# Building the expert row lists one choice at a time: both one-hot tiles on GpSimd instead of one on GpSimd and one on VectorE and ScalarE

## The reference

```python
xn = _layernorm(x)
# attention, per batch
qkv = einsum('bsd,ed->bse', xn, Wqkv_w) + Wqkv_b
scores = where(causal, einsum('bqhd,bkd->bhqk', q, k) * scale, min)
out = einsum('bsd,ed->bse', softmax(scores) @ v, out_w) + out_b
# experts, over the 2048 rows
probs = softmax(xn @ w_router.T)
top_w, top_e = top_k(probs, 4); top_w /= sum(top_w)
for e in range(16):
    coeff = sum(where(top_e == e, top_w, 0))
    ffn += coeff * ((silu(xn @ w_gate[e]) * (xn @ w_up[e])) @ w_down[e])
return x + out + ffn
```

## Time and profile before

| | us |
|---|---|
| median of 3 runs | 504.1 (502.85 to 505.03) |
| the profiled execution | 504.1 |
| its span, first to last instruction | 502.4 |
| TensorE busy | 418.8 (83%) |
| GpSimd busy | 294.8 (59%) |
| VectorE busy | 226.0 (45%) |
| ScalarE busy | 179.8 (36%) |

### The profile page before, as it was taken

The page is one execution under the profiler, slowest core; times in us unless marked ns, Lnnn a source line. Parts: engine busy times, 40 slices in busy tenths (PEclk is TensorE's granted clock), DMA queues, the critical chain, the costliest instruction groups (busy, mean ns, idle before and its releaser), DMA issues.

```text
span 502.4 us, 6742 instructions
## 1 busy us (share of the span) xinstructions
PE 418.8 (83%) x1672; PEld 227.8 (45%) x1673; DVE 226.0 (45%) x555; ACT 179.8 (36%) x424; POOL 294.8 (59%) x298
## 2 busy tenths in 40 slices
PE   4896083888889888879899999999999999999920
PEld 2242031434544544435565555555555555555510
DVE  5987688468767666413232222222222222222210
ACT  2353100337745556633333333333333333333310
POOL 7953130998511100303888888888888888888740
PEclk9889555559999999999999999999999999999985
DMA  7668796344876792642544444454544455446217
GB/s 218 228 180 189 179 131 97 126 80 136 167 151 165 179 187 86 213 147 64 78 76 81 82 79 77 77 82 76 84 74 75 84 85 82 75 77 81 38 22 146
DMA packets 54034, 57.17 MB, mean 114 GB/s; under 512 B 11376, under 2 KB 48928, under 8 KB 53760
## 3 DMA queue, kind: packets, MB, share of 16 engines
q0 software_dynamic: 15440, 21.51, 25.6%
q1 hardware_dynamic: 25904, 22.87, 20.9%
q10 hardware_dynamic: 12672, 12.58, 8.4%
HBM read 37.40 MB, written 23.33 MB: 121 GB/s over the span
## 4 chain that ended last, share of the span: by engine, by line
PE 36%; issue 19%; POOL 16%; DVE 12%; DMA 8%; SPq 4%; ACT 3%; ACTq 0%; POOLq 0%
POOL late L512 10%; PE bank L785 9%; PE bank L801 5%; PE bank L664 4%; PE bank L638 4%; PE bank L653 4%; POOL odd_d L526 3%; PE bank L692 3%; DVE pmax L1194 3%; POOL out_dram L526 3%; DMA late<-xn_d,get_row 2%; PE bank L676 2%; DVE early L1051 2%; PE bank L775 2%; DMA q_d<-early 2%
## 5 line engine op out<-in xcount | busy, mean ns | idle before, releaser
L785 PE MATMUL bank<-wgu,late 128*128 x316 | 152.2, 604 | 3.0 <-issue 1.2
L512 POOL DMA_INDIRECT late<-xn_d,get_row x79 | 83.2, 1053 | 69.2 <-PE bank L653 27.6
L1285 DVE SCALAR_TENSOR_TENSOR late<-late,bank 128x256 f32<-128x256 f32 x79 | 37.9, 480 | 154.5 <-ACT late L986 154.5
L925 ACT ACTIVATE pt<-bank 128x512 f32<-128x512 f32 x96 | 56.0, 599 | 79.3 <-PE bank L653 78.3
L801 PE MATMUL bank<-wdn,late 128*128 x316 | 81.5, 381 | 1.4 <-DVE late L1292 1.4
L1194 DVE TRANSPOSE_TENSOR_REDUCE pmax<-bank 128x16 f32<-128x512 f32 x96 | 66.5, 706 | 33.7 <-PE bank L638 32.7
L986 ACT ACTIVATE late<-bank 128x256 f32<-128x256 f32 x79 | 30.3, 383 | 130.8 <-PE bank L785 130.8
L785 PEld LDWEIGHTS bank<-wgu,late 128*128 128x128 f32 x316 | 53.7, 189 | 46.7 <-issue 45.5
L526 POOL DMA_INDIRECT out_dram<-late,slots x40 | 63.5, 1588 | 19.1 <-issue 10.4
L526 POOL DMA_INDIRECT odd_d<-late,slots x39 | 61.9, 1587 | 12.8 <-issue 9.8
L801 PEld LDWEIGHTS bank<-wdn,late 128*128 128x128 f32 x316 | 53.9, 190 | 6.4 <-issue 2.4
(11 more groups left out here) (149 smaller groups left out, 413.8 us busy)
## 6 DMA issues: line engine op xcount, KB each, us to landing
qs_late<-q_d SPq DMA_DIRECT2D x40, 128.0 KB, 4.9
q_d<-early SPq DMA_DIRECT2D x16, 256.0 KB, 3.8
wgu<-in_L_ffn_w_gate_dram ACTq DMA_DIRECT2D x8, 512.0 KB, 4.2
wgu<-in_L_ffn_w_up_dram ACTq DMA_DIRECT2D x8, 512.0 KB, 4.4
wdn<-in_L_ffn_w_down_dram ACTq DMA_DIRECT2D x8, 512.0 KB, 3.3
qs_wgu<-q_d SPq DMA_DIRECT2D x24, 128.0 KB, 4.7
xs<-in_L_attn_x_dram SPq DMA_DIRECT2D x4, 512.0 KB, 3.9
odd_d<-scan_t SPq DMA_DIRECT2D x1, 2048.0 KB, 10.6
```

What stands on the lines that cost most here:

```text
L512: pool.indirect_dma_start(xg[:, j % RING, :], None, xn_d, bass.IndirectOffsetOnAxis(ap=get_row[:, j:j + 1], axis=0), bounds_check=last_row ...
L785: mm = pe.matmul(bank[:, 2 + buf, :], xT[:, buf, c, :], wgu[:, bass.ds(e * KC + c, 1), :], start=(c == 0), stop=(c == KC - 1))
L925: act.activation(pt[:, G % 2, n % NU, :], bank[:, 3 + N % 2, :], ACT.Exp).then_inc(exp_done, 1)
L1285: dve.scalar_tensor_tensor(out=hh[:, buf, :], in0=hh[:, buf, :], scalar=xg[:, r, bass.ds(e + D, 1)], in1=bank[:, 2 + buf, F:2 * F], op0=AL ...
```

## The change

GpSimd now writes both tiles of a pair: `hot_p` as before, and `hot_j` with one `tensor_scalar` of 128x80 with two operations, is_equal and mult. `mark_tiles` on VectorE and `write_rows` on ScalarE are gone. The ring is counted in pairs (32) instead of row tiles (14 times 4). TensorE's `list_rows(n)` is one matmul, two at each step, from step 12 to step 43. `copy_k(3)`, `copy_k(4)` and `copy_k(5)` stand ahead of pair 16, 32 and 52. VectorE reads the list at step 50 instead of step 34. ScalarE's wait for the list's end stands ahead of the loads of batch 4 instead of batch 3.

```diff
-    HOTS = 14
+    NL = NT * TOP_K
+    HOTS = 32
@@ GpSimd
-            COPIES = {10: 3, HOTS: 4}
-            for t in range(NT):
-                if t in COPIES:
-                    copy_k(COPIES[t])
-                    pool.wait_ge(k_ready, 2 * COPIES[t] + 2)
-                if t >= HOTS:
-                    pool.wait_ge(list_ps, t - HOTS + 1)
-                for c in range(TOP_K):
-                    pool.tensor_scalar(hot_p[:, t % HOTS, c], iota_p[:], slot_pf[:, t, c:c + 1], None, ALU.is_equal
-                                       ).then_inc(hot_p_ready, 1)
-
-            for b in (5, 6, 7):
+            COPIES = {16: 3, 32: 4, 52: 5}
+            for n in range(NL):
+                t, c = divmod(n, TOP_K)
+                if n in COPIES:
+                    copy_k(COPIES[n])
+                    pool.wait_ge(k_ready, 2 * COPIES[n] + 2)
+                if n >= HOTS:
+                    pool.wait_ge(list_ps, n - HOTS + 1)
+                pool.tensor_scalar(hot_p[:, n % HOTS], iota_p[:], slot_pf[:, t, c:c + 1], None, ALU.is_equal
+                                   ).then_inc(hot_p_ready, 1)
+                pool.tensor_scalar(hot_j[:, n % HOTS], iota_p[:, 0:MTE], slot_jf[:, t, c:c + 1], row_no[:, t:t + 1],
+                                   ALU.is_equal, ALU.mult).then_inc(hot_j_ready, 1)
+
+            for b in (6, 7):
@@ TensorE
-            def list_rows(t):
-                pe.wait_ge(hot_p_ready, TOP_K * (t + 1))
-                pe.wait_ge(rows_written, t + 1)
-                for c in range(TOP_K):
-                    mm = pe.matmul(bank[:, 2, 0:MTE], hot_p[:, t % HOTS, c], hot_j[:, t % HOTS, c],
-                                   start=(t == 0 and c == 0), stop=(t == NT - 1 and c == TOP_K - 1), skip_group_check=True)
-                mm.then_inc(list_ps, 1)
+            def list_rows(n):
+                pe.wait_ge(hot_p_ready, n + 1)
+                pe.wait_ge(hot_j_ready, n + 1)
+                pe.matmul(bank[:, 2, 0:MTE], hot_p[:, n % HOTS], hot_j[:, n % HOTS], start=(n == 0), stop=(n == NL - 1),
+                          skip_group_check=True).then_inc(list_ps, 1)
-                    if 0 <= b * NB + s - LIST_AT < NT:
-                        list_rows(b * NB + s - LIST_AT)
+                    for n in range(2 * ((b - 1) * NB + s), 2 * ((b - 1) * NB + s) + 2):
+                        if 0 <= n < NL:
+                            list_rows(n)
@@ ScalarE
-                if b == HOT_E // (E // B) and which == 0:
-                    act.wait_ge(list_ps, NT)
+                if b == E // 2 // (E // B) and which == 0:
+                    act.wait_ge(list_ps, NL)
-            def write_rows(t):
-                act.wait_ge(hot_j_ready, t + 1)
-                act.activation(hot_j[:, t % HOTS], hot_j[:, t % HOTS], ACT.Copy, scale=row_no[:, t:t + 1]
-                               ).then_inc(rows_written, 1)
@@ VectorE
-            def mark_tiles(t):
-                if t >= HOTS:
-                    dve.wait_ge(list_ps, t - HOTS + 1)
-                if t == 0:
-                    dve.wait_ge(route_ready, 1)
-                dve.tensor_tensor(hot_j[:, t % HOTS], slot_jf[:, t].unsqueeze(2).to_broadcast([P, TOP_K, MTE]),
-                                  iota_p[:, 0:MTE].unsqueeze(1).to_broadcast([P, TOP_K, MTE]), ALU.is_equal
-                                  ).then_inc(hot_j_ready, 1)
-                    if b == 2 and s == 10:
-
-                        dve.wait_ge(list_ps, NT)
+                    if b == 4 and s == 2:
+
+                        dve.wait_ge(list_ps, NL)
```

More of the change, by code:

```diff
@@ L85, in attention_and_experts @@
         wdn = sb("wdn", [P, E * FC, D])
-        HOT_E = 6
-        hot = wgu[:, HOT_E * KC:(HOT_E + 6) * KC, :].rearrange("p r f -> p (r f)").bitcast(F16)
-        hot_p = hot[:, 0:HOTS * TOP_K * P].rearrange("p (r k c) -> p r k c", r=HOTS, k=TOP_K)
-        hot_j = hot[:, HOTS * TOP_K * P:HOTS * TOP_K * (P + MTE)].rearrange("p (r k c) -> p r k c", r=HOTS, k=TOP_K)
+        hot = wgu[:, (E // 2) * KC:(E // 2 + 4) * KC, :].rearrange("p r f -> p (r f)").bitcast(F16)
+        hot_p = hot[:, 0:HOTS * P].rearrange("p (r c) -> p r c", r=HOTS)
+        hot_j = hot[:, HOTS * P:HOTS * (P + MTE)].rearrange("p (r c) -> p r c", r=HOTS)
         xs = sb("xs", [P, NT, D])
@@ L234, in attention_and_experts @@
         hot_j_ready = sem("hot_j_ready")
-        rows_written = sem("rows_written")
         list_ps = sem("list_ps")
@@ L274, in attention_and_experts @@
         XT_BANK = [0, 6]
-        LIST_AT = NB + 2
         CHOICE_PARTS = [(0, 1), (1, 3), (3, 4)]
@@ L960, in batch @@
                     exp_scores(b, s)
-                    if 0 <= b * NB + s + 2 - LIST_AT < NT:
-                        write_rows(b * NB + s + 2 - LIST_AT)
                     if b < B - 2 and s in (3, 5, 7):
@@ L1223, in add_out @@
                 dve.tensor_tensor(tile, tile, bank[:, out_bank(b, qt), D:2 * D], ALU.add).then_inc(o_added, 1)
-            def mark_tiles(t):
-                if t >= HOTS:
-                    dve.wait_ge(list_ps, t - HOTS + 1)
-                if t == 0:
-                    dve.wait_ge(route_ready, 1)
-                dve.tensor_tensor(hot_j[:, t % HOTS], slot_jf[:, t].unsqueeze(2).to_broadcast([P, TOP_K, MTE]),
-                                  iota_p[:, 0:MTE].unsqueeze(1).to_broadcast([P, TOP_K, MTE]), ALU.is_equal
-                                  ).then_inc(hot_j_ready, 1)
             def batch(b):
                 for s in range(NB):
-                    if 0 <= b * NB + s + 4 - LIST_AT < NT:
-                        mark_tiles(b * NB + s + 4 - LIST_AT)
                     n = b * NB + s + NB + NB // 2
```

## The result

The change makes the kernel slower: 522.85 us (521.79 to 524.29, 4 runs) against 504.47 (4 runs beside them), a ratio of 1.037 with a 95% interval of 1.033 to 1.041. The forecast was 515.4 us, within 508 to 528: the direction and the mechanism are right, and the size is 7.4 us short of what came.

What follows compares the result with a forecast made beforehand. TensorE's in-order stream was taken to bound the kernel, delayed by GpSimd's longer chain: 504.1 + 10.1 delay - 0.5 recovered + 0.7 list read + 1.0 clock = 515.4 us, range 508 to 528.

Steps and rivals of the forecast that it cites:

- What bounds the kernel: TensorE, in order, bounds slices 7 to 12 (88 to 160 us); time it loses there is added to the end.
- The four lines of the sum: GpSimd's chain at 1.09 us a pair: pairs 0-15, 16-31, 32-51, 52-63 end at 105.8, 125.1, 148.5, 163.0 us; delay 10.1.
- The price J: Time of GpSimd's new two-operation 128x80 tensor_scalar: between 435 and 803 ns if like L499, taken as 500 ns.
- The 128x128 tile's own 590 ns without the marks: GpSimd's hot_p tile was taken as 590 ns, against 639 average behind 113 us, since VectorE's marks go.
- From which step TensorE starves: List products on TensorE wait for GpSimd's pairs from step 33 to 43, none before step 31, about 10 us in all.
- What comes back and what is paid again: Behind the list 0.5 us is recovered; VectorE's list read, moved to step 50, costs 0.7 us in batch 4.
- The clock: TensorE's granted clock may fall in the starving stretch, costing only behind the list: 0 to 3 us, taken as 1.
- GpSimd's instruction is dear: Rival: both operations on GpSimd cost per column, J 0.65 to 0.8 us; 527.5 us at 0.70, 534 at 0.80; chance 0.17.
- The forecast's own case: GpSimd's new instruction at J 0.4 to 0.62 us with any clock term gives 510 to 523 us; chance 0.66.
- It is cheap: Rival: GpSimd's new instruction takes 0.25 to 0.35 us, giving 507 to 510 us; chance 0.08 for 505 to 510.
- GpSimd keeps up: Rival: not slower; J at most 0.18 us, only the 1.84 us on the chain of waits counts, 502.3 us; chance 0.04.
- The clock that stays low for batches 4 and 5: Rival: TensorE's clock falls and stays low there, costing at least 3 us more a batch, 521 to 526 us; chance 0.05.

Runs made afterwards that it cites:

- The doubled: The changed kernel with the 128x80 instruction issued a second time into a scratch tile for each of the 64 pairs; 564.0 us.
- the cheapened instruction: The changed kernel with hot_j written by one operation, is_equal without the multiplication by the row's number; 512.66 us, ratio 1.017 to the kernel before.
- The probes: The kernel before with twenty GpSimd instructions of various widths and operations added behind its last copy of keys, writing to an unread scratch tile; 504.24 us.
- the fillers: The changed kernel with six unread 128-column matmuls ahead of each list product from pair 36 on, keeping TensorE busy; 520.70 us.

## Why the prediction was right, and where it was short

**What bounds the kernel: right.** TensorE's in-order stream is delayed, and nothing behind gives it back: batch 4 takes 15.13 us against 15.12, and the experts' stage is unchanged.

**GpSimd as one chain: right.** The four lines of the sum, with the measured pair of 1.205 us in place of 1.09, give 88.35 + 19.3 + 1.4 = 109.0, then 129.7, 155.2 and 169.7 us. Measured, less the 1.3 us by which the list began later: 109.0, 129.7, 155.2 and 169.7. The copies of keys found their steps done, as they do in this sum; with 1.09 the first and second would have waited a little. The doubled and the cheapened instruction follow the same line.

**The price J: the term that was mis-sized.** It was taken as 0.50 us, and it is 0.62 from start to start; with the old tile at 0.585 a pair is 1.205 us instead of 1.09. 64 x 0.115 = 7.4 us, less 0.7 us of small waits at the copies that then vanish: the delay is 16.7 us instead of 10.1, which is nearly all that the forecast lacks. The bounds from the rows, 435 to 803 ns, held it. The choice within them failed, by its reason: "most of its time in something that a second operation need not repeat". The probes show 271 ns fixed in 596, so less than half, and a second operation and its column of scalars do add 148 ns. The split from the affine selects (179 ns fixed, 3.2 a column) was near the truth for the first operation: 435 ns against 470. What was left out when choosing was the second operation, for which the same paragraph had allowed up to 256 ns. The middle of the stated bounds, 619 ns, would have given 522.

The price weighed there, the Trainium skill's best case of 1.8 cycles a column ("GPSIMD Engine Reference", section "Elementwise — side-by-side cycle accounting"), gave an estimate of 518 ns. The probes measured 2.5 ns a column for a comparison, and the second operation, of which that estimate knew nothing, makes the difference to 618.

**The 128x128 tile's own 590 ns without the marks: right.** Its longest is 668 ns in the changed kernel against 938, with a median near 597 in both. All four profiles of kernels with VectorE's marks have a tile of 825 ns or more, and none of the nine without them has one over 686. Among these nine is the kernel in which VectorE writes hot_j alone, with instructions of one tensor input: there the 24 tiles behind 113 us take 585 ns on average, against 639 before. So it is not VectorE's work as such that holds GpSimd up but the marks. That agrees with the Trainium skill, "GPSIMD Engine Reference", section "Key points", on contention with VectorE's instructions of two SBUF inputs.

**From which step TensorE starves: sooner than forecast.** Forecast was step 33, and its first wait came at the second product of step 28 (0.63 us), because GpSimd was slower and TensorE had gained 2 us in batch 1. The waits of the list's products for GpSimd's tile add up to 9.8 us, for about 10 us in all that were forecast; that is luck, since the delay is 16.7, and TensorE's own work, longer at the lower clock, filled part of it.

**What comes back and what is paid again.** I counted 0.5 us back and 0.7 us for the read of the list in batch 4. Batch 4 is equal to 0.01 us, so the read costs nothing there, and nothing visible came back.

**The clock: right in kind.** It fell, and it cost 1.0 us by the two traces and 1.5 by the fillers, for 1 us taken from a range of 0 to 3. That it costs nothing within the stretch was the forecast's reason, and the fillers show it. By the Trainium skill, "TensorE: Matmul & The Clock Gate", section "HAM oscillation", I had the upper end, 3 us; the measurement decides for half of that or less.

**The rivals.** "GpSimd's instruction is dear" began at J = 0.65, just above what it is. The forecast's own case was J up to 0.62 and 510 to 523 us, and both came at its upper edge: that it holds 522.85 is luck in part. "It is cheap" and "GpSimd keeps up" needed 0.35 and 0.18 us. The clock that stays low for batches 4 and 5 did not come: batch 4 ran at 1.00.

**What the sum had no term for.** The later start, 1.3 us in the profiled execution, and the part outside the span, 1.2 us. With them 16.7 + 1.3 + 1.0 - 0.3 + 1.2 makes the 19.9 us between the two profiled executions; a good part of the start is chance of the execution.

## What to carry to other kernels

Read an engine's free time in the stretch in which the work is due, not over the span, and follow its stream as one chain with everything that is queued on it: here 12 us of slack met 40 us of new work, and of two changes that moved the same work to two different engines, both lost time, each on an engine that had no room for it there. Price an instruction that the trace does not show by what differs from the nearest row, the second operation and its operands included, and put the value in the middle of the bounds where two rows disagree. And when work is moved to a slower engine with a stock in hand, the place where its product is wanted decides: the same instructions cost 33 us in the old order, 18 in the new one, and nothing that can be told with the consumer 19 steps later.

## What the runs showed of the hardware

- On GpSimd a comparison is dear: on 80 columns is_equal and mult took 632 ns, add and mult 406, a two-input add 314. Two per-partition columns of scalars instead of constants cost 136 ns of 618.
- TensorE at the lower of its two clock levels for half of a stretch that another engine paces costs nothing in it (62.3 us both ways), and 1.0 to 1.5 us behind it.
- GpSimd's 128x128 instruction of 597 ns took up to 825 to 941 ns in the four profiles in which VectorE ran two-input marks beside it, and at most 686 ns in the nine others, one of them with VectorE writing the same tiles by one-input instructions.
- A small DMA lands late behind large ones: of the maxima's DMAs of 16 KB the one issued 1.1 us behind a load of 512 KB, the last of six, took 6.2 us to land where the median was 2.6, and TensorE waited 2.3 us for it. With four loads spread out, the last issued 0.2 us ahead, the longest took 4.1 us, and TensorE waited 0.2 us.
- Device time holds 1.7 to 1.8 us outside the span in every run of the kernel before, and 2.9 to 3.4 us in every run of the changed one. Why was not found.
